# The setup of a macaron kernel as one row of fifteen weight units, with its norm and routing chains spread over the steps

## The reference, cut to what matters

```python
x = x + 0.5 * _L0_ffn_ref(_layernorm(x), ln_gamma, ln_beta, spline_bases, spline_slopes, output_scale)
x = x + _L0_attn_ref(_layernorm(x), Wq, bq, Wk, bk, Wv, bv, Wo, bo, rand_matrix)
x = x + 0.5 * _L0_ffn_ref(_layernorm(x), ...)
x = x + 0.5 * _L1_ffn_ref(_layernorm(x), SU_ug, SU_dp, Wscale_ug, Wscale_dp, W_up, W_gate, W_down)
x = x + _L1_attn_ref(_layernorm(x), ...)
x = x + 0.5 * _L1_ffn_ref(_layernorm(x), ...)

# _L0_ffn_ref, the routing of a token:
xn = (x - mu) * rsqrt(var + LN_EPS) * ln_gamma + ln_beta
input_sigs = sign(xn)
best_cluster = argmax(input_sigs @ cluster_sigs.T)
tile_idx = argmax(where(in_cluster, input_sigs @ tile_sigs.T, -inf))   # one of 64 tiles of 8 columns
x_slice = xn[the 8 columns of tile_idx]                                # then min and max over all tokens of the tile

# _L1_ffn_ref (fwht: a Walsh-Hadamard transform of the rows):
x = fwht(x * SU_ug) / SCALE
x = silu(x @ W_gate.T * ...) * (x @ W_up.T * ...)
x = fwht(x * SU_dp) / SCALE
x = x @ W_down.T * (Wscale_dp * SCALE)
```

## Time and profile before

| | us |
|---|---|
| median of 3 runs | 2310.25 (2309.74 to 2310.73) |
| the profiled execution | 2309.18 |
| its span | 2307.3 |
| up to the first mixed block | 46.98 |
| end of the setup's loop | 196.87 |
| first product of the attention stage (L1184) | 229.26 |
| end of the second routing (L581) | 733.38 |

### The profile page before, as it was taken

One profiled execution on the slowest core, in us unless ns is written; L12 is line 12 of the kernel. 1 busy time (PEld: TensorE's weight loads), 2 busy tenths in 40 slices (PEclk: granted clock), 3 DMA queues, 4 the chain that ended last, 5 costly groups with the idle time before them and its releaser, 6 DMA issues. The chain is left out here.

```text
span 2307.3 us, 29065 instructions
## 1 busy us (share of the span) xinstructions
PE 2010.7 (87%) x11854; PEld 945.0 (41%) x11854; DVE 1267.2 (55%) x2323; ACT 727.0 (32%) x1131; POOL 220.6 (10%) x164
## 2 busy tenths in 40 slices
PE   4784868887864899999998999989998999999998
PEld 3442323333332444444443444444444444444443
DVE  5777447576566455554565356625574466623322
ACT  4562132333321222232243223522343223412211
POOL 3630201201100000001000100001000100000000
PEclk7986878878865899999999999999999999999999
DMA  7224030302123122212111111111111111132321
GB/s 257 92 74 171 0 60 13 48 19 42 37 51 120 64 93 100 93 54 73 46 56 46 56 46 46 57 55 43 41 65 37 64 47 56 56 101 101 112 102 60
DMA packets 91136, 158.71 MB, mean 69 GB/s; under 512 B 44342, under 2 KB 55932, under 8 KB 86268
## 3 DMA queue, kind: packets, MB, share of 16 engines
q1 hardware_dynamic: 91004, 156.86, 21.4%
HBM read 128.52 MB, written 18.87 MB: 64 GB/s over the span
## 5 line engine op out<-in xcount | busy, mean ns | idle before, releaser
L1184 PE MATMUL ps<-arena 128*128 128x512 f16 (+1 forms) x4512 | 1021.8, 382 | 19.8 <-DVE arena L1965 12.9
L1184 PEld LDWEIGHTS ps<-arena 128*128 128x128 f16 x4512 | 437.4, 99 | 544.2 <-issue 57.1
L1910 PE MATMUL ps<-arena 128*128 128x512 f16 x1536 | 349.1, 383 | 29.5 <-DVE arena L1956 16.2
L1910 PEld LDWEIGHTS ps<-arena 128*128 128x128 f16 x1536 | 147.4, 98 | 207.4 <-issue 29.4
L1965 DVE SCALAR_TENSOR_TENSOR arena<-arena,ps 128x512 f32<-128x512 f32 x128 | 87.8, 686 | 210.1 <-ACT arena L1932 209.5
L1932 ACT ACTIVATE arena<-ps,arena 128x512 f32<-128x512 f32 x128 | 87.6, 684 | 362.3 <-PE ps L1184 362.1
L2517 ACT ACTIVATE arena<-ps 128x1024 f32<-128x1024 f32 (+3 forms) x128 | 90.1, 704 | 254.6 <-PE ps L2426 254.5
L2622 DVE CAST arena<-arena 128x1024 f16<-128x1024 f32 (+3 forms) x128 | 66.2, 517 | 150.6 <-ACT arena L2517 148.6
L2588 DVE TENSOR_REDUCE arena<-ps 128x2 f32<-128x256 f32 (+3 forms) x128 | 99.5, 819 | 65.1 <-PE ps L2370 65.1
L1993 DVE SCALAR_TENSOR_TENSOR arena<-ps,arena 128x512 f32<-128x512 f32 x64 | 44.0, 687 | 139.6 <-PE ps L1910 139.4
L1974 DVE SCALAR_TENSOR_TENSOR arena<-ps,arena 128x512 f32<-128x512 f32 x128 | 95.7, 748 | 39.3 <-PE ps L1184 39.1
(11 more groups left out here) (267 smaller groups left out, 2394.8 us busy)
## 6 DMA issues: line engine op xcount, KB each, us to landing
arena<-wug_dram SPq DMA_DIRECT2D x128, 512.0 KB, 3.3
arena<-wd_hi_dram SPq DMA_DIRECT2D x16, 1024.0 KB, 5.0
arena<-wd_lo_dram SPq DMA_DIRECT2D x16, 1024.0 KB, 7.2
arena<-arena SPq DMA_DIRECT2D x144, 64.0 KB, 2.1
wug_dram<-arena SPq DMA_DIRECT2D x4, 2048.0 KB, 15.8
arena<-_attn_hidden_states_dram SPq DMA_DIRECT2D x4, 1024.0 KB, 11.9
arena<-in_L_ffn_W_up_dram SPq DMA_DIRECT2D x8, 512.0 KB, 4.8
arena<-in_L_ffn_W_down_dram SPq DMA_DIRECT2D x4, 1024.0 KB, 7.3
```

The source lines that it names most:

```text
L1184: ins = pe.matmul(out, left[a](c), right[b](c), start=(at == 0), stop=(at == 3 * n - 1))
L1910: ins = pe.matmul(k.ps[:, bank, :], act[x][:, slot, cols], wd[y][:, f, :], start=(f == 0 and m == 0), stop=(f == 7 and m == 2))
```

## The change

The setup becomes one row of fifteen weight units, `WEIGHTS`: ug0, ug1, ug2, down0, ug3, ug4, down1, w0 0, ug5, down2, ug6, w0 1, down3, ug7, w0 2. There is no separate head for w0 any more. Turned tiles get three banks, and Scalar and Vector evict a mixed block one step later than TensorE makes it. The wide norm chain is gone: each chunk has its own, by the three token functions, at steps of its own (`ROUTE_UNIT` and `ROUTE_AT`; (-1, 1) is step 1 of the unit before the chunk's). GpSimd's wait for `all_chain` is gone, and blocks are scaled at the steps of `SCALE_DOWN_AT`. The mask products of the picks move to GpSimd, `route_mask_pool`, behind each mixed down block in the setup, and behind the bias in the attention stage; the second routing's picks 0 and 1 move from the end of an iteration to y = 1 of the next. SP issues loads in the new order, the eight rand_matrix DMAs early, and stores each up/gate unit when it is mixed. Cut to the core:

```diff
-def token_sums_vector(k, V, i):
+def token_sums_vector(k, V, i, new):
 
 
 
     s, e = k.s, V.eng
     for u in range(TPC):
-        e.wait_ge(s["b_bo"], TPC * i + u + 1)
+        if new:
+            if u == 0:
+                e.wait_ge(s[f"x_in{i}"], 16)
+        else:
+            e.wait_ge(s["b_bo"], TPC * i + u + 1)
         ins = e.bn_stats(k.stats6[:, u, :], k.x[:, i * TPC + u, :])
...
+def route_mask_pool(k, e, i, n):
+
+    s = k.s
+    gate(e, s["r_hot"], i + n)
+    for u in range(TPC):
+        y = k.y[:, u, :].rearrange("p (t j) -> p t j", j=DSL)
+        e.tensor_tensor(y, y, bcast(k.onehot[:, i * TPC + u, :].unsqueeze(2), [P, NTILE, DSL]), ALU.mult)\
+            .then_inc(s["r_masked"], 1)
...
     s, e = k.s, V.eng
-    gate(e, s["r_hot"], i + n)
+    gate(e, s["r_masked"], nth(i, n, TPC, u + 1))
     y = k.y[:, u, :]
-    hot = k.onehot[:, bass.ds(i * TPC + u, 1), :].squeeze(1)
-    V.link(e.tensor_tensor(y.rearrange("p (t j) -> p t j", j=DSL), y.rearrange("p (t j) -> p t j", j=DSL),
-                           bcast(hot.unsqueeze(2), [P, NTILE, DSL]), ALU.mult))
...
 UG_GROUPS = 2 * INTER // CH
-W0_GROUPS = 3
-UP_BANK = (0, 1)
+WEIGHTS = (("ug", 0), ("ug", 1), ("ug", 2), ("down", 0), ("ug", 3), ("ug", 4), ("down", 1), ("w0", 0),
+         ("ug", 5), ("down", 2), ("ug", 6), ("w0", 1), ("down", 3), ("ug", 7), ("w0", 2))
+LOADED = [n for n, (kind, at) in enumerate(WEIGHTS) if kind != "down"]
+GROUPS = len(WEIGHTS)
+MIXED = GROUPS - 3
+SCALE_DOWN_AT = ((0, 2), (2, 1), (4, 2), (7, 0))
+UP_BANK = (0, 1, 7)
 HAD_BANK = (2, 3)
...
+    def load_x(c):
+        sp.dma_start(k.x[:, c * TPC:(c + 1) * TPC, :],
+                     d["L0_attn_hidden_states"][c].rearrange("(u p) n -> p u n", p=P)).then_inc(s[f"x_in{c}"], 16)
+
+    def load_down(o):
+        if o == 3:
+            sp.wait_ge(s["nat_turned"], 4 * (WEIGHTS.index(("down", 0)) + 1))
+        sp.dma_start(k.wd_nat[:, o % 3, :], d["L1_ffn_W_down"][o * P:(o + 1) * P, :]).then_inc(s[f"wd_in{o}"], 16)
+
+    def store(n):
+        kind, g = WEIGHTS[n]
+        if kind == "ug":
+            f, which = TPC * (g % (UG_GROUPS // 2)), 1 - g // (UG_GROUPS // 2)
+            cols = slice(2 * HID * which, 2 * HID * (which + 1))
+            sp.wait_ge(s["had_lo"], 4 + 4 * (mixed_before(n) + 1))
+            sp.dma_start(d["wug"][f:f + TPC, :, cols].rearrange("f p n -> p f n"), k.wug_flat[:, f:f + TPC, cols])\
+                .then_inc(s["ug_out"], 16)
+        if kind == "down":
+            sp.wait_ge(s["wdo_lo"], 4 * (g + 1))
+            for dst, src in ((d["wd_hi"], k.wdo_hi), (d["wd_lo"], k.wdo_lo)):
+                sp.dma_start(dst[:, :, g * P:(g + 1) * P], src).then_inc(s["wdo_out"], 16)
...
+    load_nat(0)
+    load_x(0)
+    load_nat(1)
+    load_down(0)
+    load_x(1)
+    load_down(1)
     sp.wait_ge(s["rt_zeroed"], 1)
     for j in range(8):
         sp.dma_start(k.rt[32 * (j // 2):32 * (j // 2) + 32, 16 * j:16 * j + 16],
                      d["L0_attn_rand_matrix"].rearrange("e d -> d e")).then_inc(s["b_in"], 16)
-    store_down(3)
+    for n in range(GROUPS):
+        if n in LOADED and LOADED.index(n) + 2 < len(LOADED):
+            load_nat(LOADED.index(n) + 2)
+        if n < 2:
+            load_x(n + 2)
+        if n == 2:
+            load_down(2)
+        if WEIGHTS[n] == ("down", 0):
+            load_down(3)
+        if n:
+            store(n - 1)
     sp.wait_ge(s["routed"], NCH)
     sp.dma_start(k.bv, d["L0_attn_bv"].partition_broadcast(P)).then_inc(s["b_in"], 16)
     sp.dma_start(k.bo, d["L0_attn_bo"].partition_broadcast(P)).then_inc(s["b_in"], 16)
...
     s = k.s
-    e.wait_ge(s["all_chain"], 5)
     for o in range(4):
...
+        route_mask_pool(k, e, o, 1)
...
+    kind, at = WEIGHTS[n]
+    if kind == "w0":
+        c = (4 * at + r) * P
+        return (k.w0_lo if part else k.w0_hi)[:, :, c:c + P]
     side = n % 2
-    return k.wdt[side][part][:, 4 * r:4 * r + 4, :] if n % 3 == 2 else k.wt[side][part][:, :, r * P:(r + 1) * P]
-
-
-ROUTE_AT = {"stats": (0, 1), "turn": ((0, 3), (1, 0), (1, 1), (1, 2)), "sign": ((1, 0), (1, 1), (1, 2), (1, 3)),
-            "key": (2, 0), "hot": (2, 1), "pick": ((2, 1), (2, 2), (2, 2), (2, 3)), "gain": (2, 2), "ends": (3, 0)}
+    return k.wdt[side][part][:, 4 * r:4 * r + 4, :] if kind == "down" else k.wt[side][part][:, :, r * P:(r + 1) * P]
+
+
+ROUTE_UNIT = (1, 4, 7, 10)
+ROUTE_AT = {"sums": (-1, 1), "root1": (-1, 2), "first": (-1, 3), "root2": (0, 0), "second": (0, 1), "write": (0, 3),
+            "turn": ((1, 0), (1, 1), (1, 2), (1, 3)), "sign": ((1, 1), (1, 2), (1, 3), (2, 0)),
+            "key": (2, 1), "choice": (2, 2), "hot": (2, 3), "hot_out": (3, 0),
+            "pick": ((2, 3), (3, 0), (3, 0), (3, 1)), "gain": (3, 1), "ends": (3, 2)}
...
+                pe.wait_ge(s["wd_mixed"], at + 1)
             else:
-                pe.wait_ge(s["wd_mixed"], i + 1)
-        pe.wait_ge(s["wt_lo"], tile_base(n) + r - 1)
-        if g < 2:
-            native((W0_GROUPS + g) % 2, r, UP_BANK[r % 2])
+                m = LOADED.index(n)
+                pe.wait_ge(s[f"nat_in{m % 2}"], 32 * (m // 2 + 1))
+        need(pe, s["wt_lo"], 4 * n + r - 2)
+        if kind == "down":
+            turn_rows(lambda c: k.wd_nat[:, at % 3, (4 * r + c) * P:(4 * r + c + 1) * P], UP_BANK[(4 * n + r) % 3])
         else:
-            turn_rows(lambda c: k.wd_nat[:, i % 3, (4 * r + c) * P:(4 * r + c + 1) * P], UP_BANK[r % 2])
+            native(LOADED.index(n) % 2, r, UP_BANK[(4 * n + r) % 3])
 
     def mixed(n, kc):
+        kind, at = WEIGHTS[n]
...
-            if (n, r) == (GROUPS - 1, 3):
+            if (n, r) == (GROUPS, 1):
+                pe.wait_ge(s["wt_lo"], 4 * GROUPS)
                 apply_turn_tensor(k, pe, 0, 1, READY_BANK)
-    pe.wait_ge(s["had_lo"], 4 + 4 * GROUPS)
+    pe.wait_ge(s["had_lo"], 4 + 4 * MIXED)
+    pe.wait_ge(s["wt_lo"], 4 * GROUPS)
...
+            if 4 * n + r > 4:
+                mixed((4 * n + r - 1) // 4 - 1, (r - 1) % 4)
             if n < GROUPS:
                 turned(n, r)
-            if n:
-                mixed(n - 1, r)
-            i = route_now(n, r, "stats")
+            i = route_now(n, r, "root1")
             if i is not None:
-                e.wait_ge(s["r_cut"], i + 1)
-                for t in range(i * TPC, (i + 1) * TPC):
-                    ins = e.activation(k.y[:, t % TPC, :], k.x[:, t, :], ACT.Identity, bias=k.wide[6][:, t:t + 1],
-                                       scale=k.wide[5][:, t:t + 1])
-                ins.then_inc(s["z_scaled"], 1)
-                if i + 1 < NCH:
-                    scale_down(i + 1)
+                token_root_scalar(k, e, i, 1)
+            i = route_now(n, r, "root2")
+            if i is not None:
+                token_root_scalar(k, e, i, 2)
+            i = route_now(n, r, "write")
+            if i is not None:
+                e.wait_ge(s["ss_chain"], 5)
+                token_write_scalar(k, e, i)
+            if (n, r) in SCALE_DOWN_AT:
+                scale_down(SCALE_DOWN_AT.index((n, r)))
...
-    first(1)
-    setup_stats_vector(k, V)
-    setup_scale_vector(k, V)
-    first(2)
-    setup_norm_vector(k, V)
     for n in range(GROUPS + 1):
         for r in range(4):
+            if 4 * n + r > 4:
+                mixed((4 * n + r - 1) // 4 - 1, (r - 1) % 4)
             if n < GROUPS:
                 turned(n, r)
-            if n:
-                mixed(n - 1, r)
-            i = route_now(n, r, "key")
+            i = route_now(n, r, "sums")
+            if i is not None:
+                token_sums_vector(k, V, i, True)
+            i = route_now(n, r, "first")
+            if i is not None:
+                token_first_vector(k, V, i)
+            i = route_now(n, r, "second")
+            if i is not None:
...
+    if i == NCH - 1:
+        route_mask_pool(k, e, back, 1 + NCH)
     if now is not None:
         for u in range(TPC):
             e.wait_ge(s["b_res"], TPC * now + u + 1)
             xt = k.x[:, now * TPC + u, :]
             e.tensor_tensor(xt, xt, k.bo, ALU.add).then_inc(s["b_bo"], 1)
+    if back is not None and new is not None:
+        route_mask_pool(k, e, back, 1 + NCH)
...
                 mask(y)
         if i >= 2 and y in (1, 2):
-            route_pick_vector(k, V, i - 2, route, y + 1)
+            route_pick_vector(k, V, i - 2, route, 2 * y - 2)
+            route_pick_vector(k, V, i - 2, route, 2 * y - 1)
         if i >= 2 and y == 3:
...
             turn_vector(k, e, look, c, NEXT_TURN[c])
     if body:
         route_choice_vector(k, V, back, route, BACK_KEY)
-        route_pick_vector(k, V, back, route, 0)
-        route_pick_vector(k, V, back, route, 1)
     if i == NCH - 1:
         route_ends_vector(k, V, back, route, LAST_KEY)
...
         def _(sp):
             setup_sync(k, sp)
-
-            sp.wait_ge(s["had_lo"], 4 + 4 * 3 * NCH)
-            for f in range(0, FB, TPC):
```

(12 more changed lines are left out.)

243 lines of the change are left out of this document (87 added, 156 removed).

## The result

The changed kernel takes 2346.13 us (median of 4 runs, 2341.22 to 2346.37), the kernel before 2310.02 beside it: ratio 1.0152, 95% interval 1.0139 to 1.0165, so 36 us slower. The profiled execution took 2346.11 us, its span 2344.3 against 2307.3: +37.0.

A forecast was written before the change was run, and what follows sets the result against it. Setup's 197 us, limited by TensorE and VectorE, pass to the end one for one. Its end at 47.2 + 146.4 + 42 = 235.6 (+38.7), with +0.7, -1.4 and -1, gave +37 on median 2310.25: 2347 us, range 2302 to 2367.

The forecast's parts named there:

- The head: Setup's start: norm links held by GpSimd's mixing make unit 2 start at about 47.2 us instead of 34, +13.
- a stop of TensorE until about 37 to 39: Sign in setup's head that the main case is right, with first mixing in the 20s.
- The walk through units 3 and 4: Setup loop: held norm chains make the pair take 39.7 us against 25.6 undisturbed; +14 each for three pairs, +42.
- rival 2: Setup: links pass at every GpSimd stage gap, so half the blocking, 27 us instead of 55; 2319 us, chance 0.14.
- 13 + 42 = 55: Time blocked by held norm links in setup: 13 us in the head, 42 in the later groups.
- 138.1 times 1.06: Setup units 2 to 14 undisturbed: per-unit TensorE or VectorE limits sum to 138.1, times a fitted factor, 146.4 us.
- The tail: End of the attention stage: masks staggered over GpSimd and VectorE reduces take 5.4 instead of 6.8 us, -1.4.
- The attention loop: Two mask products of each of two chunks leave an iteration's end, picks become four reduces: -1, bounds -4 and +2.
- The look-up at the end of setup: TensorE's four transposes for the look-up come one eviction later, +0.7 us.
- In the setup they hide behind a step: Mask products on GpSimd, 1.05 us each, were to be hidden in setup.
- Rival 1: Norm chains run undisturbed beside GpSimd; setup ends at 180, 17 us earlier, about 2291 us in total; chance 0.13.
- Rival 3: A load or down block arrives late, stalling setup's units on GpSimd, 5 to 10 us a stall; 2370 us, chance 0.07.

The follow-up runs named there:

- e6: e5 with the picks' mask products back on VectorE, in setup and attention stage; 2318.87 us, ratio 1.0041 to the kernel before.
- e7: The changed kernel with the picks' mask products back on VectorE, nothing else undone; 2343.81 us, ratio 1.0149 to the kernel before.
- e5: The changed kernel with operands of setup's norm and ends chains placed in PSUM, plus a TensorE wait for the ends; 2294.29 us, ratio 0.9935.
- e12: The changed kernel with GpSimd mixing chunk o+1 ahead of chunk o's masks instead of behind them; 2325.07 us, ratio 1.0067.
- e11: e8 with the offsets, minima and best values of setup's ends chain in PSUM; 2292.09 us, ratio 0.9925 to the kernel before.
- e2: The changed kernel with scratch of setup's norm chains in PSUM, GpSimd's mixing untouched; 2309.46 us, ratio 1.0000 to the kernel before.
- e8: The kernel before with only the mask products moved to GpSimd; 2298.17 us, ratio 0.9951.

## Why the prediction was right, point by point

**The time.** 2347 predicted, 2346.1 measured; inside 2302 to 2367, on the side that had 0.83.

**What bounds.** The setup was the place: A is 41.0 us later, and 4.0 come back behind it. That what happens there goes into the end one for one holds within 3 us in after and the ten runs with the masks of the attention stage on GpSimd: B is 528.9 to 531.5 us and C 1571.4 to 1571.9. With these masks on VectorE (before, e6, e7) B is 532.9 to 539.1.

**The head.** Unit 2 was to start at 47.2 instead of 34. Its first product is at 47.45, and at 34.88 in e5, with free links. Of the three stops of TensorE the second and third (4.37, 4.93) are the cost of the held chain; the first (5.11) is there in e5 too (5.12). The sign "a stop of TensorE until about 37 to 39" came in another shape: the first chain was over at 32.6 and not at 36.8, because two of its six links passed in gaps, so VectorE evicted between the two chains and TensorE worked at 34.52 and stopped again until 43.20. The end is the same, since the second chain ends with the mixing (42.5, reckoned 42.8).

**The walk through units 3 and 4.** 39.7 us predicted, 39.82 measured; undisturbed 25.6 predicted, 25.80 measured in e5. The parts, from unit 3's start at 57.95: masks over at 13.25 predicted, 13.3 measured; mixing over at 32.05 and 32.1; second chain over at 32.6 and 32.5. Only the first chain was too dear, 20.3 against 18.1: L402 slips through the gap that I had seen and kept for rival 2. It gains nothing in the sum, because the second chain is held until the mixing ends in any case; the 12 us that the range gave such slips did not come. From the masks of one chunk to those of the next, after against e5: 52.4 and 38.4, 45.1 and 34.2, 49.8 and 34.6 us, so +14.0, +10.9 and +15.2: 40 for my 42.

**The held total.** I reckoned 13 + 42 = 55. After against e5 in A: 52.1.

**Where the sum was off.** The loop ended at 239.83, not 235.6. The held links were 3 us cheaper than I thought, so the rest of the loop must have been some 7 dearer: e5 shows it, its loop ends at 187.00 and not at 180. The term that was mis-sized is "138.1 times 1.06": in e5 units 2 to 14 take 152.1 us (34.88 to 187.00), which is 1.10 times 138.1. Even with free links TensorE stops three times there for 3.9 to 4.0 us at the first products of units 5, 11 and 14 and goes on at half clock (eight products in 3.59, 3.60 and 3.22 us). This may be the missing part, but no run isolates it: the granted clock is 0.83 over 12 to 188 us of e5, no lower than the 0.82 over 12 to 200 of before, which I had fitted the 1.06 to and which has stops of 3.7 and 3.4 us of its own. Two small slips in the working: 5.4 + 3.0 + 1.4 + 3.4 is 13.2 and not 13.3, and seven MB from 7.4 to 29.07 make 3.1 us a MB and not 2.8. Neither shows in the result; the first mixing began at 23.02, reckoned 22.75.

**Small terms.** The tail: -1.4 predicted, -1.7 measured (11.14 to 9.45); the staggered masks take 1.02 each, which is 1.5 times VectorE's 0.68 and not the 1.96 times that the prediction quoted. The attention loop: -1 predicted, -0.6 measured (B -2.3, less the tail's 1.7). The look-up at the end of setup: +0.7 predicted, -1.9 measured (from the end of the loop to A 4.4 us in before, 2.5 in after). TensorE's products at 196.87 in before are slow, seven in 3.35 us, after a wait of 3.19; those at 239.83 in after take 1.34 for five, after a wait of 0.94. Behind that -1.7 in C, which I had not expected. Together these came out 4.3 us better than I had them, and covered the 4.2 by which the loop ended late: the total of +37 was right to the microsecond partly because two errors met, which is luck; the mechanism and the size of the held links are not.

**What I got wrong about the masks.** "In the setup they hide behind a step" was right for VectorE and missed the queue: the masks that wait for the choice delay the mixing behind them. I did walk the mixing from the end of the masks, so the number came out, but I put the loss down to the chains standing beside GpSimd at all. e12 shows that 21 of it is the order of GpSimd's own work, which puts the mixing beside them.

**The rivals.** Rival 1's time (2291) is near what e5 measures (2294): with free links the change would have been a gain of some 15 us, though not by the new row (e11). Rival 3 did not occur: in setup TensorE waits 1.2 us for a load, and not for GpSimd. The evictions a step late and the SP queue were not undone one by one; of the edits put at 0, the third bank alone was tested by itself.

## What to carry to other kernels

In these kernels a chain of four-element instructions from SBUF to SBUF costs 0.17 us a link until it stands beside GpSimd's products; then each link costs what is left of the GpSimd instruction under way, unless it falls into a gap between two of them. Before such a chain is moved, lay GpSimd's timeline over the new place, and look at every chain that moves with it: e2 freed one and caught another. Where they must overlap, one operand of each link (or the source of a copy) in PSUM made them free, and the order of GpSimd's own queue decides where they overlap. And before the order of a stage is rewritten for speed, try the smaller parts of the change alone: e11 gained as much as e5 without it, and e8 most of that.
